# Scaled keys with the chunk and the precision half ahead of head and column instead of behind them

## What is computed

```python
def step(S, inp):
    k_t, v_t, q_t = inp
    S = lam * S
    u = beta * (v_t - jnp.einsum('kv,k->v', S, k_t))
    S = S + k_t[:, None] * u[None, :]
    o = jnp.einsum('kv,k->v', S, q_t)
    return (S, o)
...
x_act = jnp.tanh(x)                               # keys and queries
static_out = jnp.einsum('bld,ed->ble', x_act, W)  # values
y = static_out + o_dyn
...
x = _layernorm(x + attention(x));  x = _layernorm(x + ffn(x))
```

## Time and profile before

| | |
|---|---|
| median of 3 runs | 1739.97 us (1739.53 to 1741.53) |
| span of the profiled execution, first to last instruction | 1735.2 us |
| median of the runs less that span | 4.8 us |
| PE, PEld, DVE, ACT, POOL busy | 79%, 62%, 81%, 64%, 46% |
| one step (a stretch in the middle) | about 50 us |
| granted TensorE clock, mean | 0.861 |

### The profile page before, as it was taken

How to read it: one execution, slowest core, us unless ns; L and a number is a source line. 1 busy time by engine, 2 the same in 40 slices (tenths; PEclk the granted TensorE clock), 3 DMA queues, 4 the chain that set the end, 5 groups by cost and what they waited for, 6 DMA issues and landing times.

```text
span 1735.2 us, 53678 instructions
## 1 busy us (share of the span) xinstructions
PE 1378.6 (79%) x21032; PEld 1073.9 (62%) x21032; DVE 1397.8 (81%) x3461; ACT 1103.3 (64%) x2357; POOL 803.9 (46%) x1106
## 2 busy tenths in 40 slices
PE   4357888888788888887898888888888787888765
PEld 3345666666666666666666666666666666666543
DVE  5578888888888888888888888888888887888752
ACT  3235666667667666766766666676667666666654
POOL 6023454444455454544555444454544445444543
PEclk9667889988888888888889888889988888888878
DMA  4546545545545555565555656545545654555210
GB/s 122 114 104 115 111 116 115 112 111 117 118 115 118 121 113 114 116 127 108 117 119 117 112 115 126 112 118 114 120 106 116 127 109 114 119 111 114 71 34 25
DMA packets 701325, 190.98 MB, mean 110 GB/s; under 512 B 620944, under 2 KB 688528, under 8 KB 701072
## 3 DMA queue, kind: packets, MB, share of 16 engines
q1 hardware_dynamic: 701072, 187.56, 50.7%
HBM read 103.55 MB, written 67.11 MB: 98 GB/s over the span
## 4 chain that ended last, share of the span: by engine, by line
PE 32%; DVE 23%; SPq 16%; DMA 11%; ACT 10%; issue 6%; POOL 1%; ACTq 0%; POOLq 0%; DVEq 0%
PE pc L185 12%; PE pu L256 4%; DMA scr_t<-t 4%; SPq L1121 4%; SPq L1112 4%; PE pf L219 4%; ACT v L758 4%; PE pg L256 3%; PE pf L230 3%; SPq L1155 3%; SPq L1168 3%; DMA scr_x<-xt 2%; DVE S L424 2%; DVE Sp L421 2%; PE pd L282 2%
## 5 line engine op out<-in xcount | busy, mean ns | idle before, releaser
L1017 POOL TENSOR_TENSOR hlo<-gate,hhi 128x512 f16<-128x512 f32 x192 | 228.9, 1195 | 310.6 <-ACT hhi L790 310.3
L185 PE MATMUL pc<-R,tb 128*128 128x32 f16 x4096 | 158.1, 188 | 125.6 <-DVE R L407 113.1
L185 PEld LDWEIGHTS pc<-R,tb 128*128 128x128 f16 x4096 | 147.8, 118 | 141.7 <-DVE R L407 125.7
L185 PE MATMUL pc<-S,e 128*128 128x32 f16 x4096 | 157.0, 186 | 74.5 <-DVE S L428 74.5
L185 PEld LDWEIGHTS pc<-S,e 128*128 128x128 f16 x4096 | 151.3, 117 | 91.7 <-DVE S L428 84.4
L282 PE MATMUL pd<-wd_t,hhi 128*128 128x256 f16 x768 | 174.4, 274 | 15.7 <-DVE xr L526 7.9
L185 PEld LDWEIGHTS pc<-U,kb 128*128 128x128 f16 x4096 | 154.6, 118 | 46.1 <-DVE U L415 44.0
L219 PEld LDWEIGHTS pf<-xb,e 128*128 128x128 f16 x4096 | 152.3, 118 | 47.5 <-DMA e<-scr_x 29.7
L185 PE MATMUL pc<-U,kb 128*128 128x32 f16 x4096 | 159.6, 190 | 22.3 <-DVE U L415 22.3
L219 PE MATMUL pf<-xb,e 128*128 128x32 f16 x4096 | 156.3, 192 | 23.7 <-DMA e<-scr_x 22.0
L282 PE MATMUL pd<-wd_t,hlo 128*128 128x256 f16 x768 | 174.0, 274 | 0.0
(11 more groups left out here) (134 smaller groups left out, 3282.9 us busy)
## 6 DMA issues: line engine op xcount, KB each, us to landing
xa<-L_attn_x SPq DMA_DIRECT2D x128, 128.0 KB
scr_x<-xt SPq DMA_DIRECT2D x64, 256.0 KB, 2.2
xb<-scr_x SPq DMA_DIRECT2D x256, 64.0 KB, 2.9
e<-scr_x SPq DMA_DIRECT2D x256, 64.0 KB, 3.6
scr_g<-gs SPq DMA_DIRECT2D x32, 512.0 KB, 3.5
gh<-scr_g SPq DMA_DIRECT2D x32, 512.0 KB, 3.5
kb<-k SPq DMA_DIRECT2D x512, 32.0 KB, 2.2
scr_t<-t SPq DMA_DIRECT2D x64, 256.0 KB, 4.4
```

Of the source, the lines that this page charges most:

```text
L185: last = pe.matmul(pc2[:, :, cols], stationary(h, a), moving[:, :, cols], start=a == 0, stop=a == 1)
L1017: pool.tensor_tensor(hlo[:, t, :], gate[:, t % 2, :], hhi[:, t, :], ALU.subtract).then_inc(SEM["hl"], 1)
```

## The change

`k16` and `kb` get another order of their dimensions in a partition. Before, it was group, head, (sequence,) key column, half, chunk: the 128 weight columns (b, k) of one load stand 4 elements or 8 bytes apart, and the four values (half, chunk) of a key column lie side by side. After, it is group, half, chunk, head, (sequence,) key column: the 128 columns of one load are 256 bytes in a row, 2 bytes apart. The element-wise instructions that fill `k16` now read `xa` and write `k16` straight along; before they read it with a step of 256 elements inside. A contiguous run at the destination of a `kb` DMA was (key column, half, chunk), 64 elements or 128 bytes, 16 of them in each partition; now it is the 16 key columns, 32 bytes, 64 of them in each partition. The number of instructions, their order on every engine, the number of DMAs and their bytes stay the same.

```diff
-        k16 = sb("k16", [P, 2, H, DH, 2, 2], F16)
+        k16 = sb("k16", [P, 2, 2, 2, H, DH], F16)
...
-        kb = sb("kb", [P, 2, H, B, DH, 2, 2], F16)
+        kb = sb("kb", [P, 2, 2, 2, H, B, DH], F16)
...
-            pe_products(pe, lambda h, z: kb[:, w // 2, h, :, :, z, w % 2].rearrange("p b k -> p (b k)"),
+            pe_products(pe, lambda h, z: kb[:, w // 2, z, w % 2, h].rearrange("p b k -> p (b k)"),
                         U16[:, w % 2]).then_inc(SEM["sp"], 1)
...
         def dve_scale_keys(dve, q, p, g):
-            src = xa[:, 2 * g:2 * g + 2, :].rearrange("p m c -> p c m")
-            dst = k16[:, g].rearrange("p h k z m -> p z (h k) m")
+            src = xa[:, 2 * g:2 * g + 2, :]
+            dst = k16[:, g].rearrange("p z m h k -> p z m (h k)")
...
         def act_scale_keys(act, q, p, g):
-            src = xa[:, 2 * g:2 * g + 2, :].rearrange("p m c -> p c m")
-            dst = k16[:, g].rearrange("p h k z m -> p z (h k) m")
+            src = xa[:, 2 * g:2 * g + 2, :]
+            dst = k16[:, g].rearrange("p z m h k -> p z m (h k)")
...
-                sp.dma_start(kb[rows, g, :, b].rearrange("i h k z m -> i h (k z m)"),
-                             k16[rows, g].rearrange("i h k z m -> i h (k z m)")).then_inc(SEM[f"kb{g}"], 16)
+                sp.dma_start(kb[rows, g, :, :, :, b].rearrange("i z m h k -> i (z m h) k"),
+                             k16[rows, g].rearrange("i z m h k -> i (z m h) k")).then_inc(SEM[f"kb{g}"], 16)
```

More of the change, by code:

```diff
@@ L1287, in _ @@
             eng.memset(as_u32(E[1][:, :].rearrange("p z h b i n -> p (z h b i n)")), 0).then_inc(s_pool0, 1)
-            eng.memset(as_u32(kb[:, 0].rearrange("p h b k z m -> p (h b k z m)")), 0).then_inc(s_pool0, 1)
-            eng.memset(as_u32(kb[:, 1].rearrange("p h b k z m -> p (h b k z m)")), 0).then_inc(s_pool0, 1)
+            eng.memset(as_u32(kb[:, 0].rearrange("p z m h b k -> p (z m h b k)")), 0).then_inc(s_pool0, 1)
+            eng.memset(as_u32(kb[:, 1].rearrange("p z m h b k -> p (z m h b k)")), 0).then_inc(s_pool0, 1)
             eng.memset(as_u32(tb[:, :].rearrange("p g h b i z m -> p (g h b i z m)")), 0).then_inc(s_pool0, 1)
```

## The result

After the change the kernel takes 1833.47 us (median of 4 runs, 1827.45 to 1838.43) against 1740.75 us before on the same chip (1739.53 to 1745.01): a ratio of 1.052, 95% interval 1.0488 to 1.0553. It is 93 us slower. The forecast of 1727 us had the wrong sign, and the time lies above the range; it is near the figure of the third rival, descriptors handed out too slowly (1830 us).

What follows compares the result with a forecast made beforehand. No engine's rate bounds it; the chain does, spread over PE, DVE, SyncE, DMA and ACT. Less 16.3 (batches), 2.3 and 2.6 (scaled keys), plus 8.6 (kb load): 12.6 us off 1739.97 gives 1727 us, range 1711 to 1780.

Steps and rivals of the forecast that it cites:

- the third rival: kb DMAs: at 1 packet per ns a load ends over 3 us late, some 1830 us; chance 0.08.
- Weight loads: PE's kb batches: side-by-side columns make loads faster, 0.31 us per w = 1 batch, 0.19 for w = 2; 16 us less.
- The gain isn't eaten there: VectorE work behind each batch: already on the chain, so the 16 us from faster batches stay.
- Scaled keys: ACT's L705 and DVE's L441, reading straight along: 0.2 and 0.09 us shorter each time, 2.3 and 2.6 us less.
- I cost its change at nothing: SyncE's kb issue: stays 0.61 us with 1024 packets, as the gram store hands out 128 x 16 in 0.53 us.
- the 14 ns of the gram store: Second rival's kb load: at the gram store's time per packet (290 GB/s, 256-byte packets), the kernel takes about 1792 us.
- The landing: kb load for group 1 ahead of L705: 0 to 1.05 us later, 0.6 taken; kb load term 8.6 us more.
- 11 steps: Steps with group 1's kb landing on the chain: 11 x 0.6 = 6.6 us more, 2 us for the others.
- The part for fetched instructions: DMA engines during a kb load: an instruction-fetch packet may delay the landing by 0 to 0.6 us on average.
- The key store: Store scr_x behind group 0's kb load: an engine 0.45 us late is hidden by SyncE's 1.3 us idle time.
- The second: Group 1's kb load, L705, L441: above 10.2 ns a packet the load outlasts its issue, 1774 us; chance 0.25.
- the case of 11 ns: Second rival's kb load: at 11 ns a packet the kernel takes about 1755 us.

Runs made afterwards that it cites:

- alone, the layout: Changed kernel with each kb load moving the same bytes in 128-byte runs, keys landing in other columns: 1735.82 us, ratio 0.9943.
- the short runs alone: Kernel before, its layout kept, with each kb load moving the same bytes in 32-byte runs: 1840.87 us, ratio 1.0547.
- group 0 alone: Changed kernel with 32-byte runs in the kb load of group 0 only, group 1 in 128-byte runs: 1787.64 us, ratio 1.0266.
- the 55 us of group 1: Changed kernel with 32-byte runs in the kb load of group 1 only, group 0 in 128-byte runs: 1785.11 us, ratio 1.0255.

## Why the prediction was wrong, point by point

**Weight loads: right.** About 0.9 us was foretold for a batch at the full clock, 0.98 came; 0.87 for w = 2, 0.84 came, though at a clock of 0.73 in that stretch. 32 x 0.27 + 29 x 0.22 are 15 us against the 16 of the sum, and the medians over the run (0.27 and 0.19) give 14. "The gain isn't eaten there" was right of VectorE and overlooked the loop through SyncE: alone, the layout gave 10 us, PE's part included.

**Scaled keys: right in sign, too large.** L705 went from 834 to 717 ns, not 629; L441 on the chain from 0.77 to 0.75 us, not 0.68. That is 1.3 and 0.6 us by the same counts instead of 2.3 and 2.6.

**"I cost its change at nothing": the step that failed.** I took the 0.53 us in which SyncE issues the gram store for the time in which its 2048 packets are handed out. The issue ends long before that, and what is issued next pays: with 1024 packets in a DMA the median kb issue went from 0.61 to 0.73 us, SyncE issued 4.3 us longer in a step, and the short runs alone cost 95 us. A row near the true pace was there: the gram store moves 290 GB/s, in packets of 256 bytes, 1.13 a ns. I read it as what the engines can take ("the 14 ns of the gram store"), which that row alone doesn't exclude, since their share was 1.28 there, and set 206 GB/s, 1.6 packets a ns, against it. That was a stretch of 0.2 us and not a pace that lasts: in the changed kernel too up to 1.6 packets of 32 bytes a ns start within one us, while a whole kb load comes at about 1. By 1.13 a ns, 512 packets take 0.45 us and 768 take 0.68, on either side of the 0.61 us of the issue, which is where the runs found the bend.

**The landing: mis-sized.** 0 to 1.05 us later with 0.6 taken; the median is 1.2 later, and the piece on the chain 4.50 us instead of 3.22. The count "11 steps" was a property of the chain of before; after, the landing is on the chain in 26 steps. The part for fetched instructions, 0 to 0.6 us, was not tried by itself.

**The key store: the cover was gone.** I named the 1.3 us of idle time, and what happens without it, but let 0.45 us run against it. It was 3.2 us in the step shown of group 0 alone, and no more than about 1.6 us was hidden.

**The rivals.** The second named the place of group 1 rightly, yet its condition, 64 packets longer than 0.65 us on an engine, was not the one that decided: at 7.2 ns a packet, worked out below, 64 take 0.46 us. (By the terms of that rival the case of 11 ns comes to some 1743 us, not 1755; nothing rests on it.) The third, at 1 packet a ns some 1830 us, is what happened. Its chance of 0.08 rested on the argument from the 206 GB/s. The text laid its price on the landing ahead of ACT; with that wait removed the kernel is still 4.3% slower than before, some 74 us, so the way was another: a loop through SyncE, with the landing as one of its pieces. It reckoned with a landing over 3 us later, and 1.2 us were measured; that its 1830 us meets the time is luck.

**What stays open.** How the 55 us of group 1 divide between the tb load and the gram store behind it (its landing 3.5 us before, 4.7 after) was not tried apart, nor whether another queue would hand out independently. That the packets cost, and from what number on, is shown; that it is the handing out that holds them back rests on the paces below.

## What to carry to other kernels

Before making runs shorter, divide the packets of one DMA by the pace at which the trace shows packets of a long DMA coming (here some 1.1 a ns), and compare it with the time of its issue. As long as it was less here, shorter runs cost 3 to 8 us of 1740; beyond that the DMAs behind it on the queue paid too. An issue's own length doesn't tell that, the next ones' do. And what a step saved counted only on the loop that closes the step: follow the chain once round before choosing where to save.

## What the runs showed of the hardware

Packets of two sizes come at nearly the same pace from one queue. 290 GB/s in packets of 256 bytes are 1.13 a ns. In the changed kernel eight kb issues of 1024 packets each take 7.07 us in the step shown, 1.16 a ns, and inside that load (same columns as the batches above)

```profile
998.50:1004.50 6.00, 6.00 (x117) 5.24 (x116) 3.12 (x7) 3.41 (x8) 3.51 (x3) 1.00 0.59 42
```

42 GB/s in packets of 32 bytes are at most 1.3 a ns. Over the whole run the 8192 packets of a load start within 8.0 us (group 1) or 8.7 us (group 0) by the median, about 1 a ns. The engines have a share of 0.59 in the stretch above, so they are not at their limit: the share reached 1.28 in the gram store. This speaks for something ahead of the engines that sets the pace of the short packets. What it is these runs don't show, nor how the share divides among the 16 engines, nor whether the pace of the gram store has the same cause.

A 32-byte packet takes 16 x 0.59 x 32 / 42 = 7.2 ns there, against the 11.6 ns of a 128-byte packet in the kernel before (kb alone). The Trainium skill's page "DMA: Bandwidth & Descriptors" (Why small descriptors are slow) gives a fixed cost of about 3 cycles a packet beside one cycle for each 32 bytes, but for HBM only, and says that transfers between SBUF and SBUF don't suffer it. This load goes from SBUF to SBUF, and the trace doesn't agree with that exception: a quarter of the bytes takes well over half of the time. This price was not what decided.

A weight load with its columns 8 bytes apart took 118 ns on average, at 4 and at 2 bytes 102 ns, and the median batch is shorter by 22% for w = 1 and 15% for w = 2. The rule of the Trainium skill's page "SBUF — State Buffer" (Specifications), two hits in a line of 16 bytes for the full bandwidth, would have made 8 bytes as good as 2; these runs don't agree with it for weight loads.
